# A vision block on one core: order of the head, chosen rows by pairs, and who sums the image tiles

## The reference

```python
h = einsum('bcij,ce->bije', x.reshape(B,12,14,16,14,16).sum((3,5)), channel_weights)   # 64 x 196 x 192
n = layernorm(h)
attn = softmax(q k^T / 4 + causal) v  @ out_w + out_b                # 12 heads of 16, q, k, v from n
sel  = softmax((n @ sel_w + sel_b) / temperature)[..., 1]
idx  = top_k(sel, 14)                                                # 14 tokens of 196
h = h + (n, and at the rows idx: + attn * sel)
h = h + gelu(layernorm(h) @ in_weight^T + in_bias) @ out_weight
```

## Time and profile before

| | |
|---|---|
| three runs | 699.64, 708.93, 709.5 us; median 708.93 |
| the profiled execution | 706.07 us, span 704.4 us |
| busy: TensorE, VectorE | 576.7 us (82%), 522.0 us (74%) |
| busy: ScalarE, GpSimd | 335.0 us (48%), 251.9 us (36%) |
| HBM | 159 MB read, 13 MB written, 244 GB/s over the span |
| mean granted clock of TensorE | 0.942 |

### The profile page before, as it was taken

How to read it: one execution, slowest core, us unless ns; L and a number is a source line. 1 busy time by engine, 2 the same in 40 slices (tenths; PEclk the granted TensorE clock), 3 DMA queues, 4 the chain that set the end, 5 groups by cost and what they waited for, 6 DMA issues and landing times.

```text
span 704.4 us, 12381 instructions
## 1 busy us (share of the span) xinstructions
PE 576.7 (82%) x3860; PEld 475.4 (67%) x3860; DVE 522.0 (74%) x1103; ACT 335.0 (48%) x826; POOL 251.9 (36%) x484
## 2 busy tenths in 40 slices
PE   0228048899997999889998979799988999899995
PEld 0117027686976787768876777678767887788784
DVE  1767977797979888888887867988888888753411
ACT  0000044565554656554655445465645465547541
POOL 1220433444344525352535323452535253304001
PEclk9998557999999999999998989999999999999998
DMA  9996895989797979887997669797997795001001
GB/s 326 348 363 193 302 350 174 342 276 343 240 336 268 300 253 345 285 302 222 331 302 275 209 232 320 247 309 246 333 302 289 227 331 140 13 10 41 26 9 40
DMA packets 34892, 172.54 MB, mean 245 GB/s; under 512 B 3688, under 2 KB 19240, under 8 KB 22538
## 3 DMA queue, kind: packets, MB, share of 16 engines
q1 hardware_dynamic: 20224, 143.14, 56.0%
q0 software_dynamic: 6912, 11.70, 9.6%
q10 hardware_dynamic: 7690, 16.89, 6.7%
HBM read 158.99 MB, written 12.73 MB: 244 GB/s over the span
## 4 chain that ended last, share of the span: by engine, by line
PE 44%; DVE 18%; issue 16%; POOL 8%; DMA 6%; ACT 5%; POOLq 1%; DVEq 0%; SPq 0%; ACTq 0%
PE psO L637 15%; DMA X<-in_x 6%; PE psS L588 6%; DVE R L942 5%; PE psS L597 4%; PE psF L625 4%; PE psS L576 3%; PE psA L542 2%; DVE mx L1056 2%; PE psS L561 2%; ACT ET L754 2%; POOL b_ln L391 1%; DVE a_ln L952 1%; DVE b_ln L954 1%; DVE y_ln L956 1%
## 5 line engine op out<-in xcount | busy, mean ns | idle before, releaser
L942 DVE TENSOR_REDUCE R<-X 128x42 f32<-128x2688 f32 (+1 forms) x112 | 260.5, 2339 | 15.6 <-POOL X L352 8.5
L637 PE MATMUL psO<-W,act 128*112 128x192 f32 x1344 | 261.8, 339 | 11.9 <-ACT obuf L779 4.0
L637 PEld LDWEIGHTS psO<-W,act 128*112 128x112 f32 x1344 | 223.3, 183 | 18.2 <-issue 7.3
L772 ACT ACTIVATE act<-psF 128x392 f32<-128x392 f32 x192 | 95.3, 496 | 123.1 <-PE psF L625 121.2
L352 POOL TENSOR_TENSOR X<-X 128x1344 f32<-128x1344 f32 x32 | 96.9, 3027 | 21.3 <-DMA X<-in_x 21.1
L361 POOL TENSOR_TENSOR Pt<-Praw 48x196 f32<-48x196 f32 x16 | 8.6, 538 | 191.3 <-DMA Praw<-patch_sums 191.3
L625 PE MATMUL psF<-Stk,M1S 104*128 104x392 bf16 x192 | 66.1, 344 | 5.5 <-ACT act L772 4.8
L1067 DVE TENSOR_TENSOR G<-psS,K 64x336 f32<-64x336 f32 x32 | 16.0, 501 | 44.7 <-PE psS L588 44.2
L588 PE MATMUL psS<-ET,F 98*64 98x336 f32 x128 | 39.6, 452 | 10.4 <-ACT ET L754 10.4
L750 ACT ACTIVATE Sm<-Sm,rinv 112x196 f32<-112x196 f32 x96 | 35.3, 445 | 18.9 <-DVE rinv L1062 18.7
L745 ACT ACTIVATE Sm<-psS,nm 112x196 f32<-112x196 f32 x96 | 39.2, 427 | 7.3 <-DVE nm L1059 7.2
(11 more groups left out here) (197 smaller groups left out, 954.1 us busy)
## 6 DMA issues: line engine op xcount, KB each, us to landing
X<-in_x SPq DMA_DIRECT2D x96, 1344.0 KB, 8.6
X<-in_x SPq DMA_DIRECT2D x16, 672.0 KB, 4.6
X<-in_x POOLq DMA_DIRECT2D x16, 672.0 KB, 12.8
out<-obuf ACTq DMA_DIRECT2D x16, 588.0 KB, 8.7
patch_sums<-R ACTq DMA_DIRECT2D x16, 147.0 KB, 7.9
Praw<-patch_sums ACTq DMA_DIRECT2D x16, 147.0 KB, 6.5
W1T<-in_w1t ACTq DMA_DIRECT2D x1, 576.0 KB
W<-in_w ACTq DMA_DIRECT2D x1, 576.0 KB
```

The costliest lines, as they stand in the source:

```text
L637: pe.matmul(to, act_sb[u % 2][:, m, i * OT:(i + 1) * OT], W2[:, m, :], start=(m == 0), stop=False)
L772: act.activation(act_sb[u % 2][:, n // 2, (n % 2) * (GT // 2):(n % 2 + 1) * (GT // 2)], psF[:, 0:GT // 2], ACT.Gelu).then_inc(act_F1.sem, 1)
L942: dve.tensor_reduce(R[:, r, t * TQ * N:(t + 1) * TQ * N].rearrange("p (q j) -> p q j", q=TQ), v, AX.XY, ALU.add).then_inc(dve_L, 1)
```

## The change

1. *First group.* VectorE's steps for the weights no longer stand in `prepare` inside the first period but in `first_group`, with the sums of group 0 and the first two of group 1: the splitting of RS comes last, the heads after the sum of tile 6. The small selection weights are loaded before W1T, and the loads of W1T, of the attention weights and of W2 each wait for a tile of x.
2. *Chosen rows.* `rs`, `at`, `res` and `h1` are done once for two groups: ZY, G2, dsm and dsel hold both, the second at row or column 64, so the products have 120 rows. `rs` goes to another PSUM bank (psC).
3. *Tiles.* `HALVED` is (5,): GpSimd halves tile 5 alone. VectorE sums tile 0 whole, so five tiles whole and two of half size, where it was four and three.
4. *Orders.* All `plan`s but SyncE's are changed. GpSimd's has X:3 and H:5 for the group whose sums are loading, X:3 behind P; the program has one period less (`END`).

```diff
-HALVED = (0, 5)
-END = NG + 5
+HALVED = (5,)
+END = NG + 4
...
-            plan = ("X:3:1 P:s:2 c:s:5 H:5:1 A:var2:2 K:v:2 K:d1:2 K:d2:2 H:0:0").split()
+            plan = ("K:d2:2 c:s:4 P:s:1 X:3:0 H:5:0 A:var2:1 K:v:1 K:d1:1").split()
...
             def step_G(g, u, name, q):
                     if exists(g - 1):
-                        pe.wait_ge(dve_S.sem, dve_S.at(g - 1, "h1"))
+                        pe.wait_ge(dve_S.sem, dve_S.at(g - 1, "g1"))
+                    if u % 2 == 0 and exists(g - 2):
+                        pe.wait_ge(dve_Q.sem, dve_Q.at(q - 1, "h1"))
...
-                    pe.wait_ge(dve_G.sem, dve_G.at(g, "ix"))
-                    mm = pe.matmul(psS[0:SLOTS, 0, D:2 * D], ZY[:, :], BW[:, :], start=True, stop=True)
...
+            def step_rs(g, q):
+
+                pe.wait_ge(dve_G.sem, dve_G.at(g, "zy"))
+                if exists(g - 2):
+                    pe.wait_ge(dve_C.sem, dve_C.at(q - 1, "os1"))
+                pe.matmul(psC[0:PROWS, 0:D], ZY[:, :, :].rearrange("p e s -> p (e s)")[:, 0:PROWS], BW[:, :],
+                          start=True, stop=True).then_inc(pe_Q.sem, 1)
+
             def step_at(g, j):
-                mm = pe.matmul(psS[0:SLOTS, 0, 0:D], G2[:, j, :], B2[:, j, :], start=(j == 0), stop=(j == HP - 1))
+                mm = pe.matmul(psS[0:PROWS, 0, 0:D], G2[:, j, :, :].rearrange("p e s -> p (e s)")[:, 0:PROWS], B2[:, j, :],
+                               start=(j == 0), stop=(j == HP - 1))
...
# TensorE
-            plan = ("S:et:2 o:3.0:2 o:3.1:2 o:3.2:2 S:g:2 K:tr1:1 o:4.0:2 o:4.1:2 K:tr2:1 f:0:1 o:4.2:2 A:sl:1 "
-                    "at:0:2 at:1:2 f:1:1 o:5.0:2 f:2:1 at:2:2 f:3:1 A:st:1 o:5.1:2 f:4:1 G:ga:1 f:5:1 o:5.2:2 f:6:1 "
-                    "G:u:1 f:7:1 o:6.0:2 o:6.1:2 f:8:1 C:xt:2 o:6.2:2 C:fa:2 f:9:1 S:sc:1 f:10:1 C:fb:2 A:tm:0 "
-                    "f:11:1 C:f2:2 o:0.0:1 o:0.1:1 o:0.2:1 o:1.0:1 A:zt:0 o:1.1:1 o:1.2:1 o:2.0:1 o:2.1:1 o:2.2:1").split()
+            plan = ("o:2.0:2 o:2.1:2 A:zt:1 S:et:2 o:2.2:2 o:3.0:2 S:g:2 K:tr1:1 o:3.1:2 K:tr2:1 f:0:1 o:3.2:2 "
+                    "A:sl:1 at:0:2 at:1:2 at:2:2 o:4.0:2 o:4.1:2 f:1:1 o:4.2:2 f:2:1 o:5.0:2 f:3:1 A:st:1 o:5.1:2 "
+                    "f:4:1 C:xt:2 G:ga:1 f:5:1 o:5.2:2 f:6:1 G:u:1 f:7:1 C:rs:1 C:fa:2 o:6.0:2 f:8:1 S:sc:1 f:9:1 "
+                    "o:6.1:2 A:tm:0 f:10:1 o:6.2:2 f:11:1 C:fb:2 o:0.0:1 o:0.1:1 o:0.2:1 o:1.0:1 C:f2:2 o:1.1:1 "
+                    "o:1.2:1").split()
...
# ScalarE
+                act.wait_ge(x_in[0], loaded(0))
                 act.dma_start(W1T[0:DH, :, :], w1t.rearrange("(k d) n -> d k n", k=2)).then_inc(w_ffn, 16)
...
+                act.wait_ge(x_in[2], loaded(0))
                 act.dma_start(Wqkv[0:DH, :, :], wqkv.rearrange("(k d) n -> d k n", k=2)).then_inc(w_att, 16)
...
+                act.wait_ge(x_in[5], loaded(0))
+                act.dma_start(W2[:, :, :], w2.rearrange("(h p) e -> p h e", h=HT)).then_inc(w_out, 16)
...
-            plan = ("S:e0:2 S:e1:2 S:e2:2 S:e3:2 S:e4:2 S:e5:2 O:0:2 S:n:2 O:1:2 A:fm:1 K:H:1 S:t:2 K:M:1 O:2:2 "
-                    "K:L:1 A:e:1 O:3:2 R:st:0 K:k1:1 K:k2:1 f:0:1 f:1:1 f:2:1 f:3:1 O:4:2 R:ld:0 f:4:1 f:5:1 f:6:1 "
-                    "O:5:2 f:7:1 G:rs:1 C:XH:2 f:8:1 C:ga:2 f:9:1 f:10:1 O:6:2 C:gb:2 f:11:1").split()
+            plan = ("S:e1:2 S:e2:2 S:e3:2 S:e4:2 S:e5:2 O:0:2 S:n:2 O:1:2 K:H:1 S:t:2 K:M:1 A:fm:1 K:L:1 A:e:1 O:2:2 "
+                    "K:k1:1 R:st:0 K:k2:1 G:rs:2 f:0:1 O:3:2 f:1:1 f:2:1 O:4:2 f:3:1 f:4:1 R:ld:0 C:XH:2 f:5:1 f:6:1 "
+                    "f:7:1 f:8:1 O:5:2 f:9:1 C:ga:2 f:10:1 O:6:2 f:11:1 C:gb:2 S:e0:1").split()
...
# VectorE
+            def first_group():
+
+                sum_tile(0, 0, 0)
+                weights_first()
+                sum_tile(0, 0, 1)
+                weights_moments()
+                sum_tile(0, 0, 2)
+                weights_tokens()
+                sum_tile(0, 0, 3)
+                sum_tile(0, 0, 4)
+                weights_ffn()
+                sum_tile(0, 0, 5)
+                weights_parts("M")
+                sum_tile(0, 0, 6)
+                for m in range(3):
+                    weights_heads(m)
+                weights_attention("a4")
+                sum_tile(1, 1, 0)
+                weights_attention("b2")
+                sum_tile(1, 1, 1)
+                weights_parts("R")
+
-            plan = ("C:os:4 S:g:3 A:sel:2 L:0:0 A:top:2 S:at:3 A:slots:2 G:ga:2 C:xh:3 L:1:0 G:u:2 L:2:0 S:sc:2 "
-                    "A:var:1 L:3:0 S:ri:2 L:4:0 A:log:1 L:5:0 L:6:0").split()
+            plan = ("A:sel:2 S:g:3 A:top:2 C:os:4 S:at:3 C:xh:3 A:slots:2 G:ga:2 L:0:0 G:u:2 L:1:0 S:sc:2 A:var:1 "
+                    "L:2:0 S:ri:2 L:3:0 L:4:0 L:5:0 A:log:1 L:6:0").split()
```

More of the change, by code:

```diff
@@ L248, in program @@
         dve_W = Steps(sem("dve_weights"), "wr0 ws0 xh0 h10 as0 ini idb ms ms2 wcs rf mr mr2 wcr bw0 bw1 wt ws cf cf2 raw sd sd2 s1 tp tz tmm tmd tmb m1 "
-                      + " ".join(f"{n}{t}" for t in "MR" for n in splits.split()) + " q k v a4 b2 ob")
+                      + " ".join(f"{n}M" for n in splits.split()) + " q k v a4 b2 ob " + " ".join(f"{n}R" for n in splits.split()))
         block = ctx.enter_context(nc.Block())
@@ L631, in step_F2 @@
                 if m == 0:
+                    if i == 0 and isinstance(g, int) and g == 0:
+                        pe.wait_ge(w_out, 16)
+                        pe.wait_ge(dve_W.sem, dve_W.at(0, "alR"))
                     if i == 0:
@@ L653, in body @@
                         continue
-                    if stage == "C":
+                    if stage == "C" and step == "rs":
+                        if u % 2:
+                            step_rs(g, pair_of(i, k, lag))
+                    elif stage == "C":
                         if u % 2:
@@ L662, in body @@
                     elif stage == "at":
-                        step_at(g, 2 * int(step))
-                        step_at(g, 2 * int(step) + 1)
+                        if u % 2:
+                            step_at(g, 2 * int(step))
+                            step_at(g, 2 * int(step) + 1)
+                    elif stage in "GS":
+                        {"G": step_G, "S": step_S}[stage](g, u, step, pair_of(i, k, lag))
                     else:
-                        {"A": step_A, "G": step_G, "K": step_K, "S": step_S}[stage](g, u, step)
+                        {"A": step_A, "K": step_K}[stage](g, u, step)
             weights()
@@ L802, in body @@
                     else:
-                        {"A": step_A, "G": step_G, "K": step_K, "R": step_R, "S": step_S}[stage](g, u, step)
+                        {"A": step_A, "K": step_K, "R": step_R, "S": step_S}[stage](g, u, step)
             weights()
@@ L1126, in body @@
                     if stage == "L":
-                        if isinstance(i, int) and k == 0:
-                            prepare(int(step))
-                        sum_tile(g, u % 2, int(step))
+                        if not (isinstance(g, int) and (g, int(step)) < (1, 2)):
+                            sum_tile(g, u % 2, int(step))
                     elif stage == "S":
-                        stage_S(g, u, step, pair_of(i, k, lag))
+                        if step != "at" or u % 2:
+                            stage_S(g, u, step, pair_of(i, k, lag))
                     elif stage == "C":
@@ L1136, in body @@
                         {"A": stage_A, "G": stage_G}[stage](g, u, step)
[L1137 to L1139 removed]
             weights_zeroed()
+            first_group()
             periods(nc.vector, body, 8, 2)
 NW_CW = 1 + PAIRS + 2 * GB + 2
[L1146 to L1147 removed]
+NW_SEL = 3
+NW_FFN = 2
+NW_ATT = 4
 def kernel(x, L0_tok_channel_weights, L0_attn_Wqkv_w, L0_attn_Wqkv_b, L0_attn_sel_w, L0_attn_sel_b, L0_attn_out_w,
```

97 lines of the change are left out of this document (42 added, 55 removed).

## The result

The changed kernel takes 718.74 us (median of 20 runs, 705.13 to 730.26) and the kernel before 704.94 us (20 runs on the same chip, 699.64 to 710.51). The ratio is 1.0094, with a 95% interval of 1.0058 to 1.013: 0.9% slower, where 3% faster was forecast. Every ratio here is taken over the runs within 1.5% of the fastest of their kernel (7 of 20 of the changed kernel), and the medians given are over all runs, which is why those two would give 1.020 here. Each experiment is compared with runs of the kernel before on its own chip, whose median lay at 705 to 706 us. Where two experiments are set against each other, their ratios decide.

The account below looks back on a forecast made before the run. It took TensorE to bound pair periods and waiting the plain ones, and the X:3 loop (35.7 us against 36.6) to set the new period. From 706 us, -13 steady, -2.5 head and -4 tail gave 687 us, range 662 to 724.

Parts of the forecast that it names:

- take the middle, 10.1: X:3's DMA time, put between shortest 7.4 and median 12.8 us; DMA share 0.90 at old place, 0.74 at new.
- a loop through P and X:3: GpSimd issues X:3 behind the previous group's P: last sum, store, load, P, X:3, tile 3, last sum; 35.7 us.
- the first rival: X:3 takes 12.8 us in its new place, the loop 38.4: slower, 725 us; chance 0.20.
- the third: Rival: ScalarE loads the sums 10.1 us after the last sum; no steady gain, 700 to 715 us; chance 0.18.
- The plain periods wait for nm: VectorE's nm takes 2.69 us beside GpSimd's halving, 0.17 without; TensorE waits 2.63 us for what follows.
- its wait of 2.6 us should go in either case: TensorE's wait before zt goes, as zt is queued three parts of an output tile, 2 to 3 us, later.
- The remaining halving would hold nm for 1.3 us: Tile 5's halving on GpSimd would hold VectorE's nm some 1.3 us, not 2.5; bounds 0 and 3.03.
- One tile whole: +1.4 us, covered: VectorE sums tile 0 whole, 2.9 us against 1.55 halved, adding 1.4 us a group.
- `at`: 19 us for 96, no cost for 120 columns: TensorE's at falls from 192 matmuls, 37.8 us, to 96 and 19 us; growing from 56 to 120 columns costs nothing.
- Steady part -13: The 14 periods between stores of sums fall from 36.6 to 35.7 us each, the loop's time: -13 us.
- Engines alone would allow 34.1 us on average: Average period from the engines' own paths; as second rival, 664 us, chance 0.15.
- Head -2.5, bounds -7 and +2: Program start: group 0's sums complete at 54 to 58 us, group 1's at about 89 against 92.

Follow-up runs that it names:

- e2: Changed kernel with ScalarE's store of the sums moved behind k2, no longer between k1 and k2: 710.32 us, ratio 1.0068 to the kernel before.
- e15: Changed kernel with the load of the sums one gelu earlier, as in the kernel before: 711.64 us, ratio 1.0065 to the kernel before.
- e16: Kernel before with both GpSimd halvings cut to 2 elements of each row piece, so sums are incomplete: 688.83 us, ratio 0.9763.
- e17: Kernel before with only TensorE's step zt three parts of an output tile later: 702.80 us, ratio 0.9999.
- e9: e1 with tile 0 halved by GpSimd again, directly behind d2 and ahead of X:3: 700.05 us, ratio 0.986 to the kernel before.
- e1: Changed kernel with tile 3's adding DMA (X:3) issued ahead of P and the chosen rows' stores: 692.36 us, ratio 0.9839 to the kernel before.
- e10: Kernel before with tile 0 summed whole by VectorE and halved by nobody: 718.52 us, ratio 1.0203.
- e6: e1 with the products of at done for the even group too, their result overwritten: 696.01 us, ratio 0.9851 to the kernel before.
- e8: Kernel before with the new head alone (first_group and the new order of weight loads, old plans): 706.39 us, ratio 1.0016.
- e11: e1 with ScalarE's load of the sums one gelu later: 692.71 us, ratio 0.9802 to the kernel before.
- e5: Changed kernel with GpSimd's halving of tile 5 ahead of X:3, both still behind P: 745.58 us, ratio 1.0558 to the kernel before.

## Why the prediction was wrong

The direction was wrong; the time lies in the range. The step that failed is "Between the shortest and the median I find no row that is nearer, and take the middle, 10.1: the loop is 35.7 us." The mechanism, a loop through P and X:3, was right, and its other terms held or came out better, but for the pair period's store to load:

| term | forecast | plain | pair |
|---|---|---|---|
| last sum to store | 0.2 | 0.2 | 0.2 |
| store to load | 7.9 | 8.3 | 10.3 |
| load to P's end | 8.0 | 4.7 | 4.4 |
| X:3, with its issue | 10.2 | 13.9 | 15.1 |
| tile 3 to the last sum | 9.4 | 9.3 | 9.3 |
| loop | 35.7 | 36.3 | 39.3 |

X:3 was mis-sized by 3.6 to 4.8 us. In the ten periods in which VectorE waits for it, it took 13.7 to 15.6 us, not 10.1; in the other four it landed after 6.8, 7.1, 10.2 and 13.2 us. The middle was taken on the ground of the busy share, 0.90 against 0.74, and that ground does not hold. The stretch with 0.90 was not a typical one: of the 13 transfers between the head and the last group's, ten had 0.97 to 1.01 in the 12 us behind them. And in the new place the share does not tell the duration. In this order: two stretches of the kernel before, in which X:3 took 13.4 and 13.3 us, then two of the changed kernel, in which it took 14.9 and 7.1:

```profile
240.44:252.44 12.00, 11.90 (x95) 9.28 (x93) 9.07 (x39) 6.73 (x13) 1.43 (x2) 1.00 0.99 300
313.66:325.66 12.00, 11.95 (x95) 9.25 (x93) 9.07 (x39) 6.73 (x13) 1.43 (x2) 1.00 1.01 303
...
332.06:344.06 12.00, 11.49 (x76) 10.68 (x75) 11.36 (x24) 7.27 (x22) 6.37 (x11) 1.00 0.92 287
370.34:382.34 12.00, 10.61 (x57) 9.52 (x56) 9.85 (x21) 6.46 (x19) 5.84 (x9) 0.87 0.98 317
```

The argument that its issue "comes at the end of a wait, when the loads of the last tiles are through" was not borne out: in those ten periods SyncE issued one load of a tile within 1.4 us of X:3 and the next 2.3 to 4.8 us behind it.

Why the same transfer took 7 us in one period and 15 in another is not shown. One thing goes with it in the changed kernel, e2 and e15. Of their 36 transfers in periods with an output store (588 KB, on ScalarE's queue), 20 had this store issued up to 7.4 us behind X:3, and 19 of the 20 took 13.7 to 16.5 us (the other 7.8). 13 had it 7.6 us or more behind, and these took 6.8 to 11.4. No run moved that store, and in the kernel before X:3 took 11 to 15 us with no output store near it, so this is a lead and not a cause.

The load of the sums, which moves few bytes, took 2.6 us in the median where it was 6.5. Before, it went out 6.1 us behind an X:3 that took 11.7, and now no X:3 runs beside it; that this is the reason was not tested by itself. It gave most of 3.3 us back and kept the damage small.

The Trainium skill (DMA: Bandwidth & Descriptors, Anatomy of one DMA) gives 2.0 us plus the bytes at 436 GB/s; as an estimate, 3.6 us for X:3 and 2.8 for half of it. Measured were medians of 14.7 and 8.3, and no transfer under 6.8 and 5.0. By the page the loop would have bounded nothing.

So it was the first rival for the transfer (12.8 or more) and, in the pair periods, the third for ScalarE (the load 10.3 us after the store, once 12.8). Neither alone gave the time: the first forgot the shorter load, and the third priced the transfer at 9 to 10.1.

Point by point:

- *The plain periods wait for nm.* Right, and the strongest step: e16 shows 17 us for it, with what `den` adds.
- *"... and so its wait of 2.6 us should go in either case."* It went in front of zt, but e17 shows that moving zt alone moves the wait to et. It pays in the new order as a whole. Which of its other moves makes the softmax early enough was not isolated.
- *The remaining halving would hold nm for 1.3 us.* Mostly it did not: 0.28 us on average.
- *One tile whole: +1.4 us, covered.* Covered in the new order (e9 against e1), not in the old (e10).
- *`at`: 19 us for 96, no cost for 120 columns.* It was 24.0 in this profile, 19.0 in e2's. The difference is the clock, below. The forecast's saving of 2.4 us in plain periods was off the path (e6).
- *Steady part -13.* +12.6; without the loop (e1) -11.8, near the forecast's size though not by its route, which is luck.
- *"Engines alone would allow 34.1 us on average."* Not borne out: e1, which waits for no X:3 after the head, takes 36.3 us a period on average, one of them 40.4 where the loop starts again. What sets its periods was not isolated.
- *Head -2.5, bounds -7 and +2.* +2.1 by the second store. Group 0's own store came at 57.8 us, within "54 to 58", but group 1's could not follow; e8 confirms no gain.
- *Tail -4.* -5.1.
- *Not foreseen:* k2 held behind the store. The prediction named the store's own delay, "0.2", and did not ask who is queued behind it on ScalarE.

## What to carry to other kernels

An issue queued behind a wait closes a loop, and the loop can be added up from the profile. Before a transfer's new price is taken from a busy share, look at several periods: here one stretch in the old place stood at 0.90 and most of the others near 1.0, and in the new place 0.92 went with 14.9 us and 0.98 with 7.1. Where nothing tells better, a loop has to stand the long end of the rows. A wait removed is worth its length only if nothing else hangs on the same late result: making the cause small (e16) and moving one consumer (e17) are different experiments with different answers. When one order is worse than another, try the single entry with the longest wait: here one entry of GpSimd's list turns 0.9% slower into 1.6% faster than before (e1, 692.36 us); e1 and e11 (692.71) can't be told apart and are the best of all that compute the whole result.

## What the runs showed of the hardware

A wait of TensorE for k2 can cost twice. The timeline of the changed kernel, two waits of nearly the same length, and stretches around the second:

```profile
244.52 0.33 PE L530 MATMUL psA<-K,TS 98*4 98x98 f32 x2 [1.62 <-ACT Stk L746]
244.69 2.13 PE L607 MATMUL psS<-B,G 128*120 128x192 f32 x12
...
318.52 0.33 PE L530 MATMUL psA<-K,TS 98*4 98x98 f32 x2 [1.73 <-ACT Stk L746]
318.69 3.81 PE L607 MATMUL psS<-B,G 128*120 128x192 f32 x12
```

```profile
317.00:318.00 1.00, 0.00 (x0) 0.00 (x0) 0.91 (x4) 0.36 (x1) 0.00 (x0) 1.00 1.12 430
318.00:319.00 1.00, 0.48 (x4) 0.48 (x5) 0.42 (x1) 0.98 (x3) 0.00 (x0) 0.87 0.94 398
319.00:320.00 1.00, 1.00 (x5) 1.00 (x4) 0.78 (x3) 0.99 (x2) 0.00 (x0) 0.50 1.03 419
320.00:321.00 1.00, 1.00 (x5) 1.00 (x4) 0.73 (x4) 0.71 (x2) 0.00 (x0) 0.50 1.02 419
```

At 318.52 TensorE had stood still for 1.73 us, and then the granted clock was 0.50 (1.2 GHz) for about three microseconds, after the wait and not in it: the 12 matmuls of `at` took 3.81 us where they take 2.13 at full clock. So this wait of 1.7 us took 3.4 us of TensorE's time. The wait that ended at 244.52 was 0.1 us shorter and the clock stayed at 1.00. Of the nine waits of 1.6 to 1.7 us for k2 in this profile, four went with a fall to 0.50 (ending at 168, 318, 552 and 593 us; in the last two it fell already in the wait) and five with none, so the length of the wait alone does not tell. In e2, where k2 doesn't wait for the store, the same 96 matmuls take 19.0 us and not 24.0.

`nm` and `den` depend on whether GpSimd's halving runs beside them: 0.17 us alone, 2.69 beside it, and on average 0.18 and 0.17 in e16, where the halvings are short. The Trainium skill (SBUF — State Buffer, Who interferes with whom) says that VectorE and GpSimd share a port pair that one of them locks for a whole instruction, while a reduction never takes it; the sums of x keep 2.94 us everywhere, also where a halving starts inside them, which agrees. GpSimd's own halving took 3.51 us in the changed kernel, where it starts while X:3 is being issued, and 3.02 in e1 and 3.03 in e5, where it does not.
